# Attention in groups of two heads on the row halves of the tensor array, with the softmax denominators in spare columns of the value blocks

## The chip, the core and the metric

One core of one Trainium2 chip runs the kernel. Its engines are TensorE (PE: matmuls and transposes; PEld: loading of the stationary operand), VectorE (DVE), ScalarE (ACT), GpSimd (POOL) and SyncE (SP), which here only issues DMAs. The metric is the device time of one execution in microseconds; lower is better.

## What is computed

A decoder-like stack on x of shape 4 x 512 x 128: four layers, each a cross-attention to a context of 154 tokens and a feed-forward part, each with a residual and a LayerNorm ahead. The first three attentions have 16 heads of size 8; they are what the change touches.

```python
# layer 0 (layers 1 and 2: no memory keys; RMS-normed q and k, or rotary q and k)
K = concat([ctx @ Wk.T + bk, sqrt(8) * m_k])       # 154 context keys + 64 memory keys
V = concat([ctx @ Wv.T + bv, sqrt(64) * m_v])      # the value bias only on context keys
energy = einsum('bhqd,bhkd->bhqk', Qh, Kh) / sqrt(8)
energy[..., :154] = where(mask == 0, -1e20, energy[..., :154])
x = x + einsum('bhqk,bhkd->bhqd', softmax(energy), Vh) @ Wo.T + bo
```

Since the weights of a softmax add up to one, a constant vector added to all values comes out of the attention unchanged.

## The kernel before

The work is a list of 32 items in order, `ITEMS`: for each of 8 parts (A, F0, A, F1, A, F2, A3, F3) four items, one for each batch element b. A is an attention of 16 heads (layers 0, 1, 2), A3 the last attention, F0 to F3 the feed-forward parts. Every engine runs the same list in order. An item is cut into slots. `plan(i)` puts pieces for later items into the slots of item i: LayerNorm and projections of item i + 2 (`ln`, `norm`, `xt`, `q`, `kproj`), the transposed queries and keys, maxima and values of item i + 1 (`kt`, `kb`, `qxt`, `max`, `mt`, `v`), and the output projection of item i - 1 (`finish`). In a slot an engine first does the slot's own step, then the pieces in plan order. Nothing overtakes on an engine, and SP is one such queue as well: it processes `mt` (row copies), `w` (loads of feed-forward weights in chunks, at slots 4, 7, 10, ... of A items of layers 1 and 2) and `rows` in the same slot order.

An A item, before: heads are taken in 4 groups g of 4 heads. Keys lie in `KB` (97 rows: three parts of 8 for each of 4 heads, a bias row; 4 further rows for the negated maxima), queries in `QXT`, both float32r. The keys of a group are laid out as columns, head after head, cut into 7 chunks of 125 (layer 0) or 5 chunks of 124.
- `scores_for_max` (L725): 32 matmuls give scores with queries on partitions, 436 or 308 columns each, for two heads. DVE reduces each to negated maxima (`maxima`, L1100). Two PSUM banks, 2 and 3, take turns. `maxima_transposed` (L735), a copy by ACT (L1458) and four DMAs by SP (L492) bring the maxima into rows of `QXT`.
- `attention_step`: slot n computes scores of chunk n // 4 and group n % 4 with keys on partitions (L806, 512 columns) into bank n % 2; ACT exponentiates them into `P` (L1512). Four matmuls on column quarters of the array (a quad) multiply a chunk by the values into bank 6 (L817), four more by a 0/1 mask into bank 7 (L825), which gives the denominators on the same partitions as the values. There are N = 28 or 20 slots.
- `attention_end` (DVE): reciprocal of bank 7, 128 x 512 (L1219), times bank 6 (L1221). `attention_out`: output projection (L836) at slot 6 of a following A item or slot 2 of a feed-forward item, then the residual (L1228).
- `v_blocks` (L670, L673, L675): for each chunk the value projection of the context repeated four times (`ctx_rep`, loaded by a DMA for every item), a one-row matmul for the value bias, and in layer 0 the memory values.

Of the feed-forward parts, one step of F1 and F2 is two groups of three matmuls (L861 to L863) in a slot, followed by an activation on ACT and a product on DVE.

## Time and profile before

| | us |
|---|---|
| runs | 1133.59, 1137.58, 1139.87 |
| median | 1137.58 |
| profiled execution, its own time | 1143.49 |
| its span, first to last instruction | 1141.7 |
| PE busy | 1021.3 (89%) |
| DVE busy | 571.6 (50%) |
| ACT busy | 432.2 (38%) |
| POOL busy | 269.9 (24%) |

Busy time is a sum over the span; what bounds a stretch is read from that stretch. The mean granted TensorE clock was 0.918 of full speed. fp32 matmuls stand as two instructions in the trace, so a quad is eight rows.

### The profile page before, as it was taken

How to read it: one execution, taken by the hardware profiler on the slowest of the kernel's cores; microseconds unless marked ns; L12 is line 12 of the kernel's file. 1: busy time of each engine (PE TensorE's matmuls, PEld its weight loads, DVE VectorE, ACT ScalarE, POOL GpSimd, SP SyncE). 2: the span in 40 equal slices, each digit the busy share in tenths (PEclk: the TensorE clock that was granted, in tenths of full speed). 3: DMA queues.
4: the chain of work that ended last, by engine and by line, in shares of the span. 5: the costliest groups of instructions: out<-in, count | busy, mean ns of one | idle time of the engine just before them, and what ended most of it. 6: DMA issues, size and time to landing. Idle time of an engine off the chain costs nothing. (4 is left out here: it accounts for less than half of the span.)

```text
span 1141.7 us, 15533 instructions
## 1 busy us (share of the span) xinstructions
PE 1021.3 (89%) x5652; PEld 695.5 (61%) x5652; DVE 571.6 (50%) x1368; ACT 432.2 (38%) x777; POOL 269.9 (24%) x394
## 2 busy tenths in 40 slices
PE   2899999988789999989999989999989999999985
PEld 2644454336555544468887764544478888888774
DVE  3644645433345465454553445555464545444458
ACT  3164544343316445533242235553532323222240
POOL 8220112234415343310021013331210101000044
PEclk9889999787669899899999899889799999999997
DMA  5000000000010110000000011100000000000001
GB/s 137 3 1 13 1 13 2 12 1 16 1 68 1 32 31 2 30 20 1 1 1 1 1 40 43 44 25 15 26 6 1 1 1 1 1 1 1 1 1 38
DMA packets 27149, 18.11 MB, mean 16 GB/s; under 512 B 5793, under 2 KB 25345, under 8 KB 26946
## 3 DMA queue, kind: packets, MB, share of 16 engines
q1 hardware_dynamic: 27074, 17.12, 5.4%
q8 instruction: 46, 0.75, 0.3%
q14 instruction: 29, 0.24, 0.1%
HBM read 15.64 MB, written 1.05 MB: 15 GB/s over the span
## 5 line engine op out<-in xcount | busy, mean ns | idle before, releaser
L1100 DVE TENSOR_REDUCE mneg<-PS 128x2 f32<-128x308 f32 (+1 forms) x384 | 184.0, 517 | 167.7 <-PE PS L725 161.5
L1512 ACT ACTIVATE work<-PS 124x512 f32<-124x512 f32 (+1 forms) x272 | 160.1, 605 | 151.0 <-PE PS L806 150.3
L1246 DVE TENSOR_TENSOR work<-PS,work 128x512 f32<-128x512 f32 (+2 forms) x168 | 114.8, 685 | 175.4 <-PE PS L863 129.8
L1537 ACT ACTIVATE work<-PS 128x512 f32<-128x512 f32 (+2 forms) x168 | 99.9, 596 | 258.2 <-PE PS L863 245.9
L880 PEld LDWEIGHTS PS<-down_w,work 128*128 128x128 f32 (+2 forms) x1472 | 176.3, 195 | 6.3 <-DVE work L1246 1.3
L880 PE MATMUL PS<-down_w,work 128*128 128x128 f32 (+2 forms) x1472 | 176.2, 277 | 1.0 <-DVE work L1246 1.0
L861 PE MATMUL PS<-xh_sb,arena 128*128 128x512 f32 (+2 forms) x352 | 149.4, 424 | 10.4 <-DVE work L1246 9.6
L1607 POOL TENSOR_SCALAR rstd<-bn_mv 128x4 f32<-128x4 f32 x32 | 8.7, 271 | 585.3 <-DVE bn_mv L1024 585.1
L863 PE MATMUL PS<-xh_sb,arena 128*128 128x512 f32 (+2 forms) x352 | 142.5, 405 | 0.0
L862 PE MATMUL PS<-xl_sb,arena 128*128 128x512 f32 (+2 forms) x352 | 141.8, 403 | 0.0
L725 PE MATMUL PS<-kb_sb,qxt_sb 97*128 97x308 f32 x256 | 88.5, 393 | 19.8 <-DVE mneg L1100 15.6
L725 PEld LDWEIGHTS PS<-kb_sb,qxt_sb 97*128 97x128 f32 x256 | 46.8, 197 | 94.0 <-DVE mneg L1100 52.1
L861 PEld LDWEIGHTS PS<-xh_sb,arena 128*128 128x128 f32 (+2 forms) x352 | 66.1, 188 | 35.4 <-DVE work L1246 14.3
L817 PE MATMUL PS<-work,vb_sb 124*32 124x512 f32 (+1 forms) x544 | 80.3, 664 | 2.3 <-DVE work L1221 1.2
L806 PE MATMUL PS<-qxt_sb,kb_sb 101*124 101x512 f32 x160 | 74.9, 487 | 4.4 <-ACT work L1512 4.3
L863 PEld LDWEIGHTS PS<-xh_sb,arena 128*128 128x128 f32 (+2 forms) x352 | 66.1, 188 | 18.5
L825 PE MATMUL PS<-work,mv_sb 124*32 124x512 f32 (+1 forms) x544 | 76.4, 635 | 0.0
L862 PEld LDWEIGHTS PS<-xl_sb,arena 128*128 128x128 f32 (+2 forms) x352 | 66.3, 188 | 12.8
L1219 DVE RECIPROCAL work<-PS 128x512 f32<-128x512 f32 x12 | 40.3, 3357 | 43.4 <-PE PS L825 43.4
L1277 DVE SCALAR_TENSOR_TENSOR x_res<-PS,gates_sb,x_res 128x128 f32<-128x128 f32 x192 | 53.5, 339 | 5.9 <-PE PS L880 5.9
L1458 ACT ACTIVATE mt_sb<-PS 12x512 fp32r<-12x512 f32 (+1 forms) x24 | 14.1, 586 | 111.9 <-PE PS L735 111.8
L725 PE MATMUL PS<-arena,qxt_sb 97*128 97x436 f32 x128 | 48.9, 434 | 6.7 <-DVE mneg L1100 5.9
(168 smaller groups left out, 1301.6 us busy)
## 6 DMA issues: line engine op xcount, KB each, us to landing
ctx_rep<-in_ctxT SPq DMA_DIRECT2D x12, 308.0 KB, 3.3
stage<-in_w SPq DMA_DIRECT2D x8, 256.0 KB, 4.1
stage<-in_wg SPq DMA_DIRECT2D x8, 176.0 KB, 2.3
stage<-in_wu SPq DMA_DIRECT2D x8, 176.0 KB, 2.4
x_res<-in_x SPq DMA_DIRECT2D x4, 256.0 KB, 3.9
down_w<-in_w SPq DMA_DIRECT2D x1, 1024.0 KB
down_w<-in_wd SPq DMA_DIRECT2D x8, 128.0 KB
out<-x_res SPq DMA_DIRECT2D x4, 256.0 KB, 2.3
```

Of the source, the lines that this page charges most:

```text
L725: pe.matmul(PS[:, bank, 0:w], QXT[0:KX_ROWS, a % 2, g, t * 128:(t + 1) * 128], KB(layer)[0:KX_ROWS, a % 2, g, f * w:(f + 1) * w], start=Tr ...
L806: pe.matmul(PS[0:rows, n % 2, :], KB(layer)[0:K_ALL, a % 2, g, c * rows:(c + 1) * rows], QXT[0:K_ALL, a % 2, g, :], start=True, stop=True) ...
L817: pe.matmul(PS[32 * g:32 * g + 32, 6, :], VB[0:rows, a % 2, c, g * 32:(g + 1) * 32], P[0:rows, (4 * c + g) % P_RING, :], start=(c == 0), s ...
L825: pe.matmul(PS[32 * g:32 * g + 32, 7, :], mask[0:rows, c, :], P[0:rows, (4 * c + g) % P_RING, :], start=(c == 0), stop=(c == chunks - 1)). ...
L861: pe.matmul(o, w[0], xH[:, i % 2, :], start=True, stop=False)
L862: pe.matmul(o, w[0], xL[:, i % 2, :], start=False, stop=False)
L863: pe.matmul(o, w[1], xH[:, i % 2, :], start=False, stop=True).then_inc(*sig["up"].mark((i, kt, m)))
L880: mm = pe.matmul(PS[:, bank, t * 128:(t + 1) * 128], HH[0:rows, bank - 6, j, t * 128:(t + 1) * 128], rhs, start=(j == 0), stop=(j == len(t ...
L1100: dve.tensor_reduce(mneg[:, a % 2, t, h0:h0 + 2], PS[:, mx_bank(i_main, m), 0:2 * (KT0 if layer == 0 else KC)].rearrange("p (h n) -> p h n ...
L1246: dve.tensor_tensor(HH[0:rows, e % 2, j, :], PS[0:rows, 2 * (n % 2) + 1, :], SS[0:rows, n % 2, :], ALU.mult).then_inc(*sig["h"].mark((i, n)))
L1512: act.activation(P[0:rows, n % P_RING, :], PS[0:rows, n % 2, :], ACT.Exp, scale=SCALE).then_inc(*sig["p"].mark((i, n)))
L1537: act.activation(SS[0:rows, n % 2, :], PS[0:rows, bank, :], ACT.Silu).then_inc(*sig["act"].mark((i, n)))
```

## The change

Heads are taken in 8 half groups of 2 heads. Half group f of group g uses the rows 64 f to 64 f + 50 of the array (49 of them for the maxima), so that two matmuls, one on each row half, form a pair; each writes a PSUM bank of its own.

- An A item has N = 32 slots (layer 0: 4 chunks of 2 x 55 keys) or 24 (3 chunks of 2 x 52). At even slots stands a pair of scores (L851) into banks 0 and 1, and one exponential of 110 or 104 x 1024 from both (L1560). The next pair waits for it.
- Maxima: 16 pairs (L769) into banks 2 and 3 (4 and 5 in feed-forward items), one reduction of 880 or 624 values to 4 (L1148), and the next pair waits for it.
- Values: a half group has 32 columns in `VB`, 16 values, 2 columns of the mask (the denominators) and 14 zeros. One quad (L866) at every fourth slot, alternately into bank 6 and 7; no separate denominator matmuls.
- At slot N + 3 ACT evacuates both banks into `RAW` (128 x 1024, L1568). SP then issues 8 DMAs that bring the 16 denominator rows to `DEN` (128 x 64), 8 that bring the value rows to `VP`, and, after DVE's reciprocal of `DEN` (L1269), 8 that spread the reciprocals to `RB` (128 x 512). DVE multiplies `VP` by `RB` (L1275), and the output projection (L876) reads `VP`.
- In a following A item the reciprocal and its 8 DMAs stand at slot 2 (`recip`), the product at 6 (`normal`), the output projection at 8 (`finish`); in F0 at 0, 1, 2; in F1 and F2 at 1, 3, 4.
- The value bias is multiplied by the output weights once a layer (`value_bias`) and added to the output bias; the memory values have it subtracted. `ctx_rep` and its DMAs go; the context is loaded once with every column twice (`ctxR`, 128 x 1760 for 128 x 616).

```diff
-N_MAX = 2 * G * T
-P_RING = 8
-R0, C0 = 125, 7
-R1, C1 = 124, 5
...
+N_MAX = G * T
+P_RING = 4
+R0, C0 = 55, 4
+R1, C1 = 52, 3
...
         if is_attn(i - 1):
-            put(6, "finish", i - 1)
+            put(2, "recip", i - 1)
+            put(6, "normal", i - 1)
+            put(8, "finish", i - 1)
...
-            return (0, 1, 2, 3, 6, 7)[m % 6]
-        return (2 if ITEMS[i_main][0] == "A" else 4) + m % 2
+            return (0, 2, 6)[m % 3]
+        return 2 if ITEMS[i_main][0] == "A" else 4
...
+        def denominators_out(sp, i):
+            sp.wait_ge(*sig["raw"].at(i))
...
+            for j in range(2 * G):
+                bank, row = j // 4, 32 * (j % 4)
+                sp.dma_start(DEN[16 * j:16 * j + 16, :],
+                             RAW[row + 16:row + 18, bank, :].rearrange("p (s n) -> p s n", s=8)).then_inc(*sig["den_in"].more(i))
...
+            for j in range(2 * G):
+                bank, row = j // 4, 32 * (j % 4)
+                sp.dma_start(VP[16 * j:16 * j + 16, :], RAW[row:row + 16, bank, :]).then_inc(*sig["v_in"].more(i))
+        def reciprocals_out(sp, i):
+            sp.wait_ge(*sig["rden"].at(i))
...
+            for d in range(HD):
+                sp.dma_start(RB[d:128:HD, :].rearrange("p (s n) -> p s n", s=8), DEN[:, :]).then_inc(*sig["rden_in"].more(i))
...
+                    for f in range(2):
+                        if f in taken:
+                            pe.wait_ge(*taken[f])
+                        taken[f] = sig["p"].at((i, m))
+                    for f in range(2):
+                        mm = pe.matmul(PS[0:HB * rows, f, :], chunk_columns(layer, a % 2, g, f, c),
+                                       QXT[HALF * f:HALF * f + K_ALL, a % 2, g, :], start=True, stop=True)
...
-        def attention_end(i):
...
-            dve.reciprocal(ON, PS[:, 7, :]).then_inc(*sig["rden"].mark(i))
-            dve.tensor_tensor(ON, PS[:, 6, :], ON, ALU.mult).then_inc(*sig["on"].mark(i))
+        def reciprocals(i):
+            dve.wait_ge(*sig["den_in"].at(i))
+            dve.reciprocal(DEN[:, :], DEN[:, :]).then_inc(*sig["rden"].mark(i))
+        def normalise(i):
+            dve.wait_ge(*sig["v_in"].at(i))
+            dve.wait_ge(*sig["rden_in"].at(i))
+            dve.tensor_tensor(VP[:, :], VP[:, :], RB[:, :], ALU.mult).then_inc(*sig["on"].mark(i))
```

SP's queue, from the row copies for the third item of layer 1 (`qxt_sb<-mt_sb`) to its weight chunks (`stage<-in_w_1`). Before:

```order
L492 DMA qxt_sb<-mt_sb 4x512 x4
L485 DMA ctx_rep<-in_ctxT 128x4x154
L507 DMA stage<-in_w_1 128x512 x2
L492 DMA qxt_sb<-mt_sb 4x512 x4
L485 DMA ctx_rep<-in_ctxT 128x4x154
L507 DMA stage<-in_w_1 128x512 x2
```

Of the change:

```order
L503 DMA qxt_sb<-mt_sb 2x512 x8
L512 DMA den_sb<-raw_sb 16x1x64 x8
L518 DMA v_packed<-raw_sb 16x512 x8
L526 DMA rden_rows<-den_sb 16x8x64 x8
L541 DMA stage<-in_w_1 128x512 x2
L503 DMA qxt_sb<-mt_sb 2x512 x8
```

The weight chunks of an item stood behind its predecessor's row copies and one load; now 24 DMAs stand between.

PE, at the head of the second item of layer 1, up to behind the output projection of the item before it. Before:

```order
L650 MATMUL PS<-ident_sb,kx_sb 97x77 x8
L806 MATMUL PS<-qxt_sb,kb_sb 124x512 x2
L709 MATMUL PS<-ident_sb,qx_sb 97x128 x4
...
L806 MATMUL PS<-qxt_sb,kb_sb 124x512
L817 MATMUL PS<-work,vb_sb 32x512 x4
L725 MATMUL PS<-kb_sb,qxt_sb 128x308 x2
L806 MATMUL PS<-qxt_sb,kb_sb 124x512
L725 MATMUL PS<-kb_sb,qxt_sb 128x308 x2
L836 MATMUL PS<-w_attn,work 128x128 x4
L806 MATMUL PS<-qxt_sb,kb_sb 124x512
```

Of the change:

```order
L685 MATMUL PS<-ident_sb,kx_sb 115x78 x8
L851 MATMUL PS<-qxt_sb,kb_sb 104x512 x2
L749 MATMUL PS<-ident_sb,qx_sb 115x128 x4
...
L866 MATMUL PS<-work,vb_sb 32x512 x4
L769 MATMUL PS<-kb_sb,qxt_sb 128x312 x2
L851 MATMUL PS<-qxt_sb,kb_sb 104x512 x2
L769 MATMUL PS<-kb_sb,qxt_sb 128x312 x4
L851 MATMUL PS<-qxt_sb,kb_sb 104x512 x2
L769 MATMUL PS<-kb_sb,qxt_sb 128x312 x2
L876 MATMUL PS<-w_attn,v_packed 128x128 x4
L866 MATMUL PS<-work,vb_sb 32x512 x4
```

The output projection stands behind five pairs of scores (0 to 4) and four pairs of maxima, where it stood behind seven single scores and four maxima; seven pairs of scores follow it in the item.

DVE, in the same place, from the value mask to the residual. Before:

```order
L1052 TENSOR_TENSOR vb_sb<-PS,mv_sb 124x128
L1219 RECIPROCAL work<-PS 128x512
L1221 TENSOR_TENSOR work<-PS,work 128x512
L1022 BN_STATS bn_st<-x_res 128x6
L1024 BN_AGGR bn_mv<-bn_st 128x2
```

Of the change:

```order
L1269 RECIPROCAL den_sb<-den_sb 128x64
L1061 BN_STATS bn_st<-x_res 128x6
L1063 BN_AGGR bn_mv<-bn_st 128x2
L1148 TENSOR_REDUCE mneg<-PS 128x4 x2
L1275 TENSOR_TENSOR v_packed<-v_packed,rden_rows 128x512
L1148 TENSOR_REDUCE mneg<-PS 128x4 x2
L1282 TENSOR_TENSOR x_res<-PS,x_res 128x512
```

Reciprocal and product stood together ahead of the next item; now two maxima stand between them and two behind them, in the middle of the item.

## Rows read from the trace of the kernel before

**Rows 1.** The page: the span, and part 1, busy us, share and instructions.

```profile
span 1141.7 us, 15533 instructions
...
PE 1021.3 (89%) x5652; PEld 695.5 (61%) x5652; DVE 571.6 (50%) x1368; ACT 432.2 (38%) x777; POOL 269.9 (24%) x394
```

**Rows 2.** Windows, an attention item each: length; busy PE, PEld, DVE, ACT, POOL; PEclk, DMA.

```profile
58.70:108.30 49.60, 46.75 (x269) 25.10 (x270) 21.68 (x38) 23.58 (x44) 7.38 (x9) 0.95 0.03 8
108.30:157.40 49.10, 45.48 (x270) 23.34 (x269) 26.91 (x48) 23.59 (x43) 7.39 (x9) 1.00 0.03 8
157.40:208.00 50.60, 46.67 (x250) 22.14 (x248) 26.26 (x50) 22.18 (x41) 12.53 (x24) 0.93 0.03 8
208.00:240.70 32.70, 29.49 (x143) 9.79 (x142) 11.71 (x19) 17.52 (x33) 12.64 (x24) 0.84 0.01 2
...
342.20:384.00 41.80, 39.34 (x209) 21.64 (x209) 20.89 (x50) 20.23 (x37) 19.09 (x38) 0.87 0.07 21
384.00:424.50 40.50, 37.85 (x209) 20.18 (x209) 23.25 (x55) 20.14 (x38) 19.07 (x38) 0.91 0.02 5
424.50:462.10 37.60, 33.75 (x189) 16.29 (x187) 20.82 (x47) 18.61 (x35) 9.52 (x13) 1.00 0.07 22
462.10:484.60 22.50, 20.39 (x107) 8.71 (x106) 11.25 (x25) 13.69 (x28) 9.67 (x13) 0.85 0.12 38
...
679.40:722.00 42.60, 39.63 (x196) 20.08 (x197) 19.47 (x41) 20.58 (x40) 14.85 (x18) 0.84 0.24 69
722.00:762.00 40.00, 37.80 (x209) 20.14 (x209) 23.17 (x51) 20.84 (x40) 15.74 (x19) 0.91 0.07 18
762.00:802.80 40.80, 37.25 (x185) 17.06 (x183) 20.63 (x46) 18.59 (x35) 7.10 (x8) 0.89 0.11 33
802.80:824.90 22.10, 21.52 (x103) 9.09 (x102) 10.84 (x24) 13.60 (x29) 7.80 (x9) 0.74 0.07 17
```

**Rows 3.** Groups by line and shape: busy us, mean ns, idle before.

```profile
L1100 DVE TENSOR_REDUCE mneg<-PS 128x2 f32<-128x308 f32 x256 | 111.5, 473 | 114.8 <-PE PS L725 109.5
L1100 DVE TENSOR_REDUCE mneg<-PS 128x2 f32<-128x436 f32 x128 | 72.5, 605 | 52.9 <-PE PS L725 52.0
L817 PE MATMUL PS<-work,vb_sb 124*32 124x512 f32 x320 | 48.7, 683 | 1.2 <-DVE work L1221 0.6 <-ACT work L1512 0.5
L673 PE MATMUL PS<-b_v,ind_sb 1*124 1x128 f32 x80 | 22.9, 372 | 0.0
```

**Rows 4.** Timeline: start, duration us, engine, line; end of layer 0, then 418.74.

```profile
236.79 0.73 PE L806 MATMUL PS<-qxt_sb,arena 101*125 101x512 f32 x2
237.32 1.08 ACT L1512 ACTIVATE work<-PS 125x512 f32<-125x512 f32 x2 [0.57 <-PE PS L806]
...
237.45 1.07 PE L817 MATMUL PS<-work,vb_sb 125*32 125x512 f32 x8
...
238.44 0.73 PE L806 MATMUL PS<-qxt_sb,arena 101*125 101x512 f32 x2
...
418.74 1.93 PE L817 MATMUL PS<-work,vb_sb 124*32 124x512 f32 x8
```

**Rows 5.** SP's issues: one tile's (ns, min/median/max), then the timeline, and who waits.

```profile
L492 SPq DMA_DIRECT2D qxt_sb<-mt_sb x48: 584/585/700, 53.8 to 799.7; - x48
...
255.15 0.58 SPq L515 DMA_DIRECT2D qb_sb<-xn_sb  x1
255.78 0.58 SPq L516 DMA_DIRECT2D qb_sb<-xn_sb  x1
...
257.46 1.03 POOL L1713 TENSOR_TENSOR stage<-qb_sb,eye_sb 4x512 f32<-4x512 f32 x1 [3.55 <-DMA qb_sb<-xn_sb]
```

**Rows 6.** The page, part 6: weight chunks, KB and us from issue to landing.

```profile
stage<-in_wg SPq DMA_DIRECT2D x8, 176.0 KB, 2.3
```

**Rows 7.** Timeline: around the end of layer 1's last attention item.

```profile
484.60 1.06 PE L817 MATMUL PS<-work,vb_sb 124*32 124x512 f32 x8 [0.54 <-ACT work L1512]
...
492.96 1.06 PE L836 MATMUL PS<-w_attn,work 128*128 128x128 f32 x8
```

More of the change, by code:

```diff
@@ L99, in weight_chunks, with last_pair, last_quad, last_attention @@
     return [(m, e * F2, F2) for e in range(E2) for m in range(2)] + [(m, E2 * F2, FS) for m in range(2)]
+def last_pair(i):
+    return n_slots(i) // 2 - 1
+def last_quad(i):
+    return n_slots(i) // 4 - 1
+def last_attention(i):
+    return max(n for n in range(i) if ITEMS[n][0] == "A")
 def last_expert(kind):
@@ L139, in plan @@
                 put(0, "kt", a1)
-            for h in range(HL):
+            for h in range(HB):
                 put(h, "kb", a1, h)
@@ L180, in plan @@
             put(0, "kt", a1)
-            for h in range(HL):
+            for h in range(HB):
                 put(0, "kb", a1, h)
@@ L655, in v_blocks @@
[L655 removed]
+                taken[4] = taken[5] = sig["kb"].at((a, HB - 1))
+            def v_blocks(a):
                 layer, b = a // B, a % B
                 rows, chunks = chunk_shape(layer)
[L659 to L673 removed]
+                if a == 0:
+                    pe.wait_ge(*sig["mem_ready"].at(0))
+                    pe.wait_ge(*sig["const_in"].at(0))
+                pe.wait_ge(*taken[4])
+                for c in range(chunks):
+                    o = PS[0:HB * rows, 4, c * D:(c + 1) * D]
+                    cols = slice(c * HB * rows, (c + 1) * HB * rows)
+                    mem = layer == 0 and (c + 1) * rows > KP
+                    mm = pe.matmul(o, ctxR[:, b, cols], WA[:, layer % 2, 2, :], start=True, stop=not mem)
@@ L809, in attention_step @@
                 if n % 4 == 1 and n >= 5:
[L810 to L811 removed]
+                    u = (n - 5) // 4
+                    c, bank = u // 2, 6 + u % 2
+                    pe.wait_ge(*sig["p"].at((i, 2 * u + 1)))
                     if c == 0:
[L813 to L818 removed]
@@ L819, in attention_step @@
-                if n % 4 == 3 and n >= 7:
-                    c = (n - 7) // 4
-                    mask = MV0 if layer == 0 else MV1
-                    if c == 0 and 7 in taken:
-                        pe.wait_ge(*taken[7])
-                    for g in range(G):
-                        pe.matmul(PS[32 * g:32 * g + 32, 7, :], mask[0:rows, c, :], P[0:rows, (4 * c + g) % P_RING, :],
-                                  start=(c == 0), stop=(c == chunks - 1)).then_inc(*sig["dn"].mark((i, 4 * c + g)))
-                    if c == chunks - 1:
-                        taken[6] = taken[7] = sig["on"].at(i)
+                        if u == 0:
+                            pe.wait_ge(*sig["vb"].at(a))
@@ new lines, in attention_step @@
+                        if bank in taken:
+                            pe.wait_ge(*taken[bank])
+                        taken[bank] = sig["raw"].at(i)
+                    for r in range(4):
+                        j = 4 * (u % 2) + r
+                        mm = pe.matmul(PS[32 * r:32 * r + 32, bank, :], VB[0:HB * rows, a % 2, c, j, :], P[0:HB * rows, j // 2, j % 2, :],
+                                       start=(c == 0), stop=(c == chunks - 1))
+                    mm.then_inc(*sig["pv"].mark((i, u)))
@@ L1566, in _ @@
             q_split(0)
-            for h in range(HL):
+            for h in range(HB):
                 kb_out(0, h)
```

478 lines of the change are left out of this document (235 added, 243 removed).

## The prediction

> **What bounds the kernel now.** I read the page's busy times first, then the windows cut at the first exponential of each attention item, then the groups by shape, then two short pieces of the timeline. TensorE is busy for 1021.3 of 1141.7 us [rows 1]; no other engine passes 50%. The twelve attention items take 470 us of the span [rows 2]: 49 to 51 us each in layer 0, 38 to 43 us in layers 1 and 2, and the last item of each layer, which carries no maxima for a following attention, 32.7, 22.5 and 22.1 us up to its last exponential. Inside them TensorE is busy over 90% of the time while DVE and ACT stand at about half: there TensorE's instruction stream is the bound, and DVE and ACT have room. SP issues four small DMAs for an item and is idle otherwise. The last item of a layer is different: [rows 4] shows two scores at 236.79, their exponentials from 237.32 for 1.08 us, and the next two scores at 238.44. That is a loop of 1.65 us through ACT, not TensorE's own work.
>
> **What the change takes off TensorE.** (a) Denominator products (L825) go, and the value products become quads of 4 matmuls over 110 or 104 keys: layer 0 has 8 quads where 7 + 7 stood, layers 1 and 2 have 6 where 5 + 5 stood. A quad takes 1.0 us ([rows 4], 1.07 with its tail; the 40 value quads of layers 1 and 2 in [rows 3] are 48.7 us of busy time, 1.2 each, slow ones among them). That is 6 us less for an item of layer 0 and 4 us for the others, 56 us in all. (b) Value projection: the bias rows (L673, two instructions of 0.29 us each in [rows 3]) go, and there are 4 or 3 blocks instead of 7 or 5: some 5 and 3 us an item, 44 us. (c) 32 maxima matmuls become 16 pairs on row halves, 28 or 20 score matmuls become 16 or 12 pairs. Whether halves run side by side no row shows: a pair costs between one matmul and two. I take one and a bit (0.3 to 0.4 us), since the groups of four on column quarters, the nearest case in the trace, do overlap [rows 4]. So about 100 us of TensorE work leave the attention items without doubt. If nothing replaced it, this would be the gain.
>
> **Loop lengths that take its place.** Every pair now fills both banks it has, so nothing is double-buffered. Scores to exponentials: 0.53 + up to 1.08 (1024 columns in one instruction; it may save 0.1) + 0.04 = 1.55 to 1.65 us a pair [rows 4]: 16 x 1.6 = 25.6 us in layer 0, 12 x 1.6 = 19.2 us in the others, against 14 x 1.65 and 10 x 1.65 before. Maxima: one reduction over 880 or 624 values. From 0.473 us for 308 and 0.605 us for 436 [rows 3] each value adds 1.03 ns, giving 1.06 and 0.80 us; with about 0.5 us from matmul to reduction (as scores to exponentials) and 0.04 back the loop is 1.6 and 1.35 us, and 16 of them are 26 and 22 us. ACT also has 2 key copies and 4 query copies at an item's head, so the first maxima come some 7.5 us in, and after the last one stand the value blocks, a quad and two groups of transposes, 3.5 to 4.5 us. Undisturbed, an item with maxima is then 7.5 + 15 x 1.35 + about 1.5 (projections queued between the maxima) + 3.5 = 33 us in layers 1 and 2, and 7.5 + 15 x 1.6 + 2 + 4.5 = 38 us in layer 0. Only the first item of each layer is undisturbed: 49.6 to 38, 41.8 and 42.6 to 33: **-30 us**.
>
> **What the change adds to the path.** The denominators no longer leave PSUM through one DVE reciprocal but through SP: 8 DMAs for denominators, 8 for the values, 8 for the reciprocals, all queued on SP in this order (the first order piece of the section on the change). An SBUF-to-SBUF issue holds SP for 0.584 to 0.585 us and the next starts 0.63 us after it [rows 5]; the last of a set has landed 1.7 us after its issue begins (255.78 to 257.46). Counted from the end of the evacuation, T: denominators issued by T+5.0, landed T+6.2, reciprocal done T+6.6; values issued until T+10.1, and only then SP reaches the reciprocals, whose last issue begins at T+14.5 and lands at T+16.2; the product (0.69, as L1221 before) is done at T+17. The next item's first score stands about 1.1 us before T, since the evacuation (up to 1.08 us) waits behind a 4-row copy on ACT. TensorE wants this product at slot 8, ahead of pair 5, which it reaches about 10 us into the item. **It waits there until about 18 us.** Queued behind it are all later scores, maxima and quads; ACT and DVE then wait for those. DVE meets the same chain earlier: its reciprocal stands at slot 2, its product at slot 6 behind two maxima, so nothing of DVE's can help. In layers 1 and 2 SP's weight loads for slots 4 and 7 (second order piece) now stand behind the reciprocals: issued at T+15.1, landed about 2.3 later [rows 6], copied by ACT by 19 us into the item. Exponential 3 and those behind it wait for that, so pair 4 starts at 20 us.
>
> **The sum, item by item.**
> - Layer 0, second and third: slot 8 at 18.1, one product of 0.8, 13 maxima x 1.6, queued work of 2.3, tail 4.5: 46.5 each against 49.1 and 50.6: **-7**.
> - Layers 1 and 2, second and third: 20 + 13 x 1.35 + 3 + 3.5 = 44 each against 40.5, 37.6, 40.0 and 40.8: **+17**.
> - Last items: layer 0 18.1 + 0.8 + 1 + 11 x 1.6 = 37.5 against 32.7; the others 20 + 0.5 + 8 x 1.6 = 33 against 22.5 and 22.1 (first score to last exponential): **+5 and +21**.
> - The FFN items that follow them: their copy of this wait stands at slot 2 (F0) or 4 (F1, F2). Before, the output projection came 6 to 8 us after the last exponential (492.96 against 484.60 [rows 7]); now T is 2.2 us after it and the wait ends at 19. F0 +13; in F1 and F2 two more steps of FFN matmuls, 3 us, run ahead of it: +8.5 each: **+30**.
> - F0 and F1 items that prepare an attention: half the maxima matmuls and fewer value blocks, but single-buffered: -6. Prologue: 17 us of reductions for 19.4, shorter value projection, larger context load ahead of the weights: -3 (between -6 and +3). **-9**.
>
> Sum: -30 - 7 + 17 + 26 + 30 - 9 = +27 us against the profiled execution's 1141.7 (1143.5 with what lies around it), 1169 for the same span. The median of the runs shown is 1137.6, 5.9 below that execution, so I forecast **1165 us**. The value bias moved into the output bias costs one matmul and one small addition a layer, at an item's start: nothing.
>
> **One rule weighed.** [rows 5] shows each issue at 0.58 us, one after the other, for four rows of 0.5 to 2 KB: eight of them cost 5 us before the last has begun. The Trainium skill, "DMA: Bandwidth & Descriptors", section "Issuing engines are not separate DMA queues", says that the sequencer time to initiate a DMA "is usually small relative to the DMA itself". By that rule the three sets would cost little more than three landings, about 6 us, which is rival 1. The trace speaks against it.
>
> **Rivals.** (1) **The chain is hidden.** Were issues cheap, the product would be ready 6 us after T, before slot 8: no item would be held, all would run at 38 and 33 us, the last ones at 26.5 and 20: -30 - 24 - 27 - 11 + 3 - 9 = -98, about 1040 us. It decides at the issue time: twelve chains share the +27, so a chain 2.3 us shorter (0.53 us an issue for 0.63) is break-even. Against it stand 48 issues between 584 and 700 ns [rows 5]. (2) **TensorE's queue is quicker than I reckon**, each loop 0.2 us shorter because exponential and reduction of double width save more of their fixed part: about 150 loops, -30 us, 1135 us. Nothing in the trace has these widths. (3) **Issues of many short rows cost more**: the reciprocal DMAs move 128 pieces of 256 bytes; 0.25 us more on 16 of the 24 is 4 us on twelve chains, +48, 1213 us. (4) **Row halves do not overlap, or the clock is low after each 8 us pause**: a quad took 1.93 us at 418.74 [rows 4] where it takes 1.07 at the full clock; +0.15 us on each loop, or 2 to 3 us after each of twelve pauses, is about +30, 1195 us.
>
> **How the numbers follow.** Forecast 0.52 (1140 to 1190 by the bounds above), rival 1 0.10, rival 2 and the lower edge of the forecast 0.18, rival 3 0.10, rival 4 0.10. The range 1115 to 1210 leaves out rival 1 and the upper part of rival 3. Within 0.5%, about what a measurement here can tell from no change, is 1132 to 1143: 0.13. Faster: rival 1 and half of rival 2, 0.22. Slower: 0.65.
>
> **What would show it.** Right: SP busy with 24 issues of 0.63 us after each attention item; TensorE idle 6 to 8 us before the output projection in 9 attention items and 3 FFN items, released by DVE's product, which was released by a DMA; first items of layers at 38 and 33 us; the granted clock at 1.2 GHz for a while behind each pause. Wrong: issues of 0.3 us or less, an output projection that waits for nothing, or score pairs that follow each other in under 1.4 us.

## The result and the profile after the change

The changed kernel takes 1274.3 us (median of 4 runs, 1269.8 to 1281.2) against 1137.2 us (median of 4 runs) on the same chip: a ratio of 1.121, 95% interval 1.115 to 1.127. The forecast was 1165 us, up to 1210. The sign was right, and the loss (137 us) is five times the 28 us that were forecast. Some runs of any of these kernels fall into a slower state with a lower granted clock; comparisons are between the others, of which e9_split has only one.

From the page of the changed kernel (span 1279.4 us): each engine's busy time, the granted clock in 40 slices (tenths of full speed), and the chain that ended last.

```profile
PE 988.2 (77%) x5034; PEld 651.6 (51%) x5034; DVE 518.2 (41%) x1167; ACT 439.6 (34%) x649; POOL 263.0 (21%) x375
PEclk9566666657855665568999995665558999999997
PE 60%; SPq 15%; DVE 11%; ACT 5%; issue 5%; DMA 3%; POOL 1%; DVEq 0%; ACTq 0%; POOLq 0%
```

Two things stand out. SP's queue is 15% of the chain (the page of the kernel before follows its own chain back over 1 or 2% of the span only, so there is no share to set beside it). And the granted clock, 7 to 9 tenths in all but two slices before, is 5 to 7 tenths wherever attention items run. TensorE's busy time fell by only 33 us (1021.3 to 988.2), though by the forecast's count about 100 us of work were taken from it: what is left takes longer.

The windows of the changed kernel, cut as in [rows 2], columns as there. Four of layer 0, the stretch of FFN0, four of layer 1, the stretch of FFN1, and from the last item of layer 2 to the end.

```profile
53.60:105.80 52.20, 44.48 (x199) 20.86 (x200) 20.04 (x26) 24.07 (x31) 5.61 (x7) 0.62 0.00 1
105.80:164.70 58.90, 43.83 (x199) 19.87 (x198) 22.13 (x30) 23.92 (x32) 7.38 (x9) 0.62 0.05 11
164.70:222.70 58.00, 39.92 (x176) 17.09 (x174) 23.13 (x32) 22.04 (x28) 12.53 (x24) 0.62 0.05 11
222.70:266.50 43.80, 28.77 (x106) 9.05 (x106) 8.88 (x21) 18.08 (x21) 12.59 (x23) 0.59 0.06 14
266.50:384.10 117.60, 71.56 (x315) 50.25 (x315) 37.30 (x80) 27.67 (x45) 36.06 (x53) 0.69 0.04 9
384.10:429.40 45.30, 39.63 (x167) 19.82 (x168) 18.24 (x34) 21.17 (x29) 18.99 (x38) 0.55 0.10 36
429.40:483.30 53.90, 35.35 (x167) 17.22 (x167) 19.73 (x37) 20.67 (x29) 19.14 (x38) 0.65 0.08 21
483.30:536.00 52.70, 37.64 (x146) 16.48 (x146) 17.18 (x29) 19.36 (x26) 9.55 (x13) 0.52 0.08 21
536.00:574.10 38.10, 19.65 (x86) 8.18 (x86) 7.16 (x19) 14.44 (x19) 9.17 (x12) 0.61 0.11 29
574.10:768.20 194.10, 174.45 (x1058) 147.10 (x1058) 93.38 (x235) 62.00 (x99) 22.04 (x23) 0.97 0.02 6
...
916.70:956.80 40.10, 22.12 (x82) 8.16 (x82) 8.03 (x18) 15.08 (x21) 7.81 (x9) 0.50 0.13 33
956.80:1279.40 322.60, 294.77 (x1764) 248.47 (x1764) 163.75 (x466) 96.20 (x175) 39.11 (x44) 0.96 0.02 6
```

Every attention item is longer than before, the undisturbed first ones too (52.2 against 49.6, 45.3 against 41.8), at a clock of 0.50 to 0.65 where [rows 2] has 0.74 to 1.00. A granted clock of 0.50 is the lower of TensorE's two levels, 1.2 GHz, all the time, and 1.00 the higher, 2.4 GHz. The FFN1 stretch and the last one run close to the higher one (0.97 and 0.96), and FFN0 has 0.69; the same stretches of the kernel before have 0.96, 0.97 and 0.72.

The chain of DMAs is where the forecast put it. The second item of layer 1 starts at 429.4; its timeline, some rows left out (start, duration, engine and line, in brackets the idle time before and who ended it):

```profile
429.84 5.31 SPq L512 DMA_DIRECT2D den_sb<-raw_sb  x8
...
435.20 5.00 SPq L518 DMA_DIRECT2D v_packed<-raw_sb  x8
...
436.30 0.55 DVE L1269 RECIPROCAL den_sb<-den_sb 128x64 f32<-128x64 f32 x1 [9.28 <-DMA den_sb<-raw_sb]
...
440.30 5.09 SPq L526 DMA_DIRECT2D rden_rows<-den_sb  x8
445.43 1.06 SPq L541 DMA_DIRECT2D stage<-in_w  x2
446.77 0.69 DVE L1275 TENSOR_TENSOR v_packed<-v_packed,rden_rows 128x512 f32<-128x512 f32 x1 [7.44 <-DMA rden_rows<-den_sb]
...
448.49 0.63 ACT L1513 ACTIVATE arena<-stage 128x512 fp32r<-128x512 f32 x1 [12.92 <-DMA stage<-in_w]
...
450.18 0.75 PE L851 MATMUL PS<-qxt_sb,kb_sb 51*104 51x512 f32 x2 [8.12 <-ACT work L1560]
```

The 24 issues fill SP from 429.84 to 445.39, the product is done at 447.46, 17.6 us after they began; the weight load, queued behind them, lets ACT go on at 448.49, and TensorE has waited 8.1 us for the exponential behind that copy.

What the forecast did not have is in the loops. From the first item of layer 1, where no chain disturbs (rows in between left out):

```profile
393.03 0.63 PE L769 MATMUL PS<-kb_sb,qxt_sb 49*128 49x312 f32 x2
...
404.70 0.41 PE L769 MATMUL PS<-kb_sb,qxt_sb 49*128 49x312 f32 x2
...
406.10 0.41 PE L769 MATMUL PS<-kb_sb,qxt_sb 49*128 49x312 f32 x2 [0.75 <-DVE mneg L1148]
406.44 1.06 PE L866 MATMUL PS<-work,vb_sb 104*32 104x512 f32 x8
...
409.60 0.63 PE L769 MATMUL PS<-kb_sb,qxt_sb 49*128 49x312 f32 x2 [0.68 <-DVE mneg L1148]
...
411.22 0.63 PE L769 MATMUL PS<-kb_sb,qxt_sb 49*128 49x312 f32 x2 [0.34 <-DVE mneg L1148]
...
411.78 1.93 PE L866 MATMUL PS<-work,vb_sb 104*32 104x512 f32 x8
411.89 0.81 DVE L1148 TENSOR_REDUCE mneg<-PS 128x4 f32<-128x624 f32 x1 [0.81 <-PE PS L769]
...
413.65 0.63 PE L769 MATMUL PS<-kb_sb,qxt_sb 49*128 49x312 f32 x2
...
422.95 0.63 PE L769 MATMUL PS<-kb_sb,qxt_sb 49*128 49x312 f32 x2 [1.00 <-DVE mneg L1148]
```

The reduction takes 0.81 us, as reckoned (0.80). The two row halves run side by side: two matmuls in 0.41 us, no longer than the one of before. But from 407 us on a pair takes 0.63 us and a quad 1.93 instead of 1.06. The loop of 1.40 us (404.70 to 406.10; 1.35 was reckoned) becomes 1.62 (409.60 to 411.22), and 2.43 us (411.22 to 413.65) where a quad stands in it: at 1.06 us the quad lies beside DVE's work (after the one at 406.44 the next pair still waits 0.36 us for DVE), at 1.93 it sticks out by 0.8. The first and the last row are the first and the sixteenth pair of maxima of the item: 15 loops in 29.9 us.

### The profile page after: what moved, and what is told of

It reads as the page before. It is cut to its first block, busy times and chain, and to the rows that moved or that the text cites. A ratio compares the mean times of both kernels' runs of the same rounds, so it can differ in the third digit from the quotient of the medians.

```text
span 1279.4 us, 14562 instructions
## 1 busy us (share of the span) xinstructions
PE 988.2 (77%) x5034; PEld 651.6 (51%) x5034; DVE 518.2 (41%) x1167; ACT 439.6 (34%) x649; POOL 263.0 (21%) x375
## 4 chain that ended last, share of the span: by engine, by line
PE 60%; SPq 15%; DVE 11%; ACT 5%; issue 5%; DMA 3%; POOL 1%; DVEq 0%; ACTq 0%; POOLq 0%
PE PS L920 13%; PE PS L866 9%; DVE mneg L1148 6%; PE PS L901 6%; PE PS L769 6%; PE PS L903 6%; PE PS L902 6%; SPq L512 5%; SPq L518 5%; SPq L526 4%; PE PS L851 4%; ACT work L1560 2%; PE PS L876 2%; PE PS L779 1%; PE PS L702 1%
## 5 line engine op out<-in xcount | busy, mean ns | idle before, releaser
L1148 DVE TENSOR_REDUCE mneg<-PS 128x4 f32<-128x624 f32 (+1 forms) x192 | 170.6, 894 | 205.4 <-PE PS L769 205.2
L1560 ACT ACTIVATE work<-PS 104x1024 f32<-104x1024 f32 (+1 forms) x160 | 163.5, 1022 | 185.7 <-PE PS L851 184.0
L866 PE MATMUL PS<-work,vb_sb 104*32 104x512 f32 (+1 forms) x640 | 140.5, 967 | 3.4 <-ACT work L1560 3.4
L851 PE MATMUL PS<-qxt_sb,kb_sb 51*104 51x512 f32 x192 | 62.8, 642 | 74.0 <-ACT work L1560 72.4
L769 PE MATMUL PS<-kb_sb,qxt_sb 49*128 49x312 f32 x256 | 69.1, 527 | 60.1 <-DVE mneg L1148 54.5
L769 PEld LDWEIGHTS PS<-kb_sb,qxt_sb 49*128 49x128 f32 x256 | 36.0, 259 | 127.8 <-DVE mneg L1148 94.9
L851 PEld LDWEIGHTS PS<-qxt_sb,kb_sb 51*104 51x104 f32 x192 | 23.7, 230 | 105.5 <-ACT work L1560 91.3
L876 PE MATMUL PS<-w_attn,v_packed 128*128 128x128 f32 x96 | 24.8, 440 | 45.1 <-DVE v_packed L1275 30.9
L769 PE MATMUL PS<-arena,qxt_sb 49*128 49x440 f32 x128 | 38.3, 600 | 25.0 <-DVE mneg L1148 25.0
```

The lines of the kernel that those rows point to most:

```text
L769: mm = pe.matmul(PS[:, bank + f, 0:w], QXT[half, a % 2, g, t * 128:(t + 1) * 128], KB(layer)[half, a % 2, g, 0:w], start=True, stop=True)
L851: mm = pe.matmul(PS[0:HB * rows, f, :], chunk_columns(layer, a % 2, g, f, c), QXT[HALF * f:HALF * f + K_ALL, a % 2, g, :], start=True, sto ...
L866: mm = pe.matmul(PS[32 * r:32 * r + 32, bank, :], VB[0:HB * rows, a % 2, c, j, :], P[0:HB * rows, j // 2, j % 2, :], start=(c == 0), stop= ...
L1148: dve.tensor_reduce(mneg[:, a % 2, t, g * HL:(g + 1) * HL].rearrange("p (f h) -> p f h", f=2), PS[:, bank:bank + 2, 0:HB * head_width(laye ...
L1560: act.activation(P[0:rows, m % P_RING, :, :], PS[0:rows, 0:2, :], ACT.Exp, scale=SCALE).then_inc(*sig["p"].mark((i, m)))
```

## The experiments

Eleven kernels, each beside runs of the kernel before on its own chip. "Ratio" is against those.

**1. The chain moved later (e1_late).** The changed kernel with other slot numbers for the chain, and for the weight loads that queue behind it on SP:

```diff
-            put(2, "recip", i - 1)
-            put(6, "normal", i - 1)
-            put(8, "finish", i - 1)
+            put(10, "recip", i - 1)
+            put(16, "normal", i - 1)
+            put(18, "finish", i - 1)
...
-                put(4 + 3 * (c - b * n_w // B), "w", layer, c)
+                put(9 + 3 * (c - b * n_w // B), "w", layer, c)
...
-            put(0 if short else 1, "recip", i - 1)
-            put(1 if short else 3, "normal", i - 1)
-            put(2 if short else 4, "finish", i - 1)
+            put(0 if short else 2, "recip", i - 1)
+            put(4 if short else 8, "normal", i - 1)
+            put(5 if short else 10, "finish", i - 1)
```

> The changed kernel with its chain of DMAs moved later, nothing left out: in an attention item the reciprocal stands at slot 10, the product at 16 and the output projection at 18 (2, 6 and 8 before), the weight loads of layers 1 and 2 begin at slot 9 instead of 4; in the FFN entries product and projection stand at slots 4 and 5 (F0), 8 and 10 (F1, F2). Theory A (the chain of 24 SP issues holds TensorE, as forecast): the held items shrink to the length of the first item of their layer: layer 0 58.9 and 58.0 to 52, layer 1 54.0 and 52.7 to 45, layer 2 53.4 and 50.8 to 44, last items 43.8, 38.1, 40.1 to 37, 31, 31, FFN entries 5 us each: 85 us less, about 1190 us; still 50 us over the kernel before, since the undisturbed items are 3 us too long even then. Theory B (the loops and a TensorE clock at its lower level set the length, the chain mostly lies beside them): held work comes back elsewhere, not more than 30 us less, 1245 us. If the clock follows TensorE's share of busy time, taking the pauses away raises the granted clock above 0.6 in these items and the gain passes 100 us.

Measured: 1189.2 us (1181.8 to 1190.8), ratio 1.045 (1.036 to 1.053), 85 us less than the changed kernel. Windows of this kernel: first item of layer 0, first and second of layer 1, last of layer 1, the FFN1 stretch.

```profile
53.90:103.30 49.40, 41.70 (x199) 19.99 (x200) 20.40 (x28) 24.06 (x31) 7.16 (x10) 0.66 0.00 1
...
354.50:399.70 45.20, 39.52 (x167) 19.73 (x168) 18.62 (x36) 21.22 (x29) 20.63 (x41) 0.55 0.10 36
399.70:443.90 44.20, 32.14 (x167) 16.05 (x168) 19.86 (x37) 20.73 (x30) 18.17 (x38) 0.73 0.11 26
...
489.20:519.80 30.60, 22.44 (x86) 8.74 (x86) 5.02 (x17) 14.59 (x19) 7.33 (x10) 0.55 0.14 36
519.80:701.30 181.50, 170.94 (x1058) 144.80 (x1058) 93.64 (x235) 61.80 (x99) 22.13 (x23) 1.00 0.02 6
```

The second item of layer 1 falls from 53.9 to 44.2, about the length of the undisturbed first; the last from 38.1 to 30.6; FFN1 from 194.1 to 181.5. Theory A holds: the chain costs the change at least 85 us. At least, because it has not left the path everywhere. In this same second item TensorE still waits 4.8 us (up to 427.67) for an exponential that stands behind a weight chunk queued on SP behind the reciprocals, in FFN0 5.7 us (up to 265.47) for the product, and the second item of layer 2 takes 52.7 us, hardly less than in the changed kernel (53.4), where 44 had been expected. The run also says that the chain is not all: 1189 is some 50 us above the kernel before (by the ratio; the runs that it is compared with have a median of 1140.4), and the first item of layer 1 did not change (45.3 and 45.2).

**2. The values' copies on the POOL queue (e5_vpool).** The eight issues of a set go to another queue, the chain stays at its slots:

```diff
-                    sp.dma_start(VP[16 * j:16 * j + 16, :], RAW[row:row + 16, bank, :]).then_inc(*sig["v_in"].more(i))
+                    pool.dma_start(VP[16 * j:16 * j + 16, :], RAW[row:row + 16, bank, :]).then_inc(*sig["v_in"].more(i))
```

> The changed kernel, nothing left out, with the chain at its slots but the eight copies of the values issued from the POOL queue instead of SP's. Theory A (the 24 issues one after the other on SP set when the product is ready): SP reaches the reciprocals 5 us earlier, product at about T+12 instead of T+17, the weight loads 5 us earlier: 5 us less on nine held attention items and three FFN entries, 60 us less than the changed kernel's 1274 (or 45 where a part of it is taken up by other waits): 1215 to 1230 us. Theory B (the landings set it, not the issues, or POOL issues slower than SP): within 15 us of the changed kernel. If an issue on POOL costs 1.1 us instead of 0.63, the eight take 9 us and still end before T+12: nothing is lost unless POOL's own work is late.

Measured: 1234.9 us (1228.9 to 1236.7), ratio 1.085 (1.078 to 1.092): 39 us less. The timeline of its second item of layer 0:

```profile
99.52 4.13 POOL L1764 DMA_DIRECT2D v_packed<-raw_sb  x8 [5.29 <-ACT raw_sb L1563]
99.56 5.29 SPq L512 DMA_DIRECT2D den_sb<-raw_sb  x8
...
106.59 5.46 SPq L521 DMA_DIRECT2D rden_rows<-den_sb  x8
...
113.42 0.69 DVE L1270 TENSOR_TENSOR v_packed<-v_packed,rden_rows 128x512 f32<-128x512 f32 x1 [2.88 <-DMA rden_rows<-den_sb]
```

The reciprocals' issues begin 7.0 us after the first issue, and the product ends at 14.6 us. The same item of the changed kernel has 11.1 and 18.2 us. In the second item of layer 1 the product ends at 14.6 us again, 17.6 in the changed kernel. 3.0 to 3.6 us less on twelve chains is 36 to 43 us, about what was measured. I had reckoned 5: SP is free after 5.3 us, but then waits for DVE's reciprocal, which the longer queue had hidden. So the issues, one after the other, are the greater part of the price of this chain: 15.5 of the 17.6 us in the changed kernel.

**3. One part of the change alone (e4_bias).** The kernel before, with the value bias joined to the output bias and nothing else:

```diff
-                    pe.matmul(o, CR[:, a % 2, cols], WA[:, layer % 2, 2, :], start=True, stop=False)
-                    ind = IND0[:, cols] if layer == 0 else IND0[:, 0:rows]
-                    mm = pe.matmul(o, ind, BVr[:, layer, :], start=False, stop=not mem)
+                    mm = pe.matmul(o, CR[:, a % 2, cols], WA[:, layer % 2, 2, :], start=True, stop=not mem)
...
+                pe.matmul(PS[:, 5, 0:D], BVc[:, layer:layer + 1].to_broadcast([128, 128]), WA[:, layer % 2, 3, :],
+                          start=True, stop=True).then_inc(*sig["bv_psum"].mark(layer))
```

> The kernel before with one part of the change alone: the value bias goes into the output bias (one matmul and one addition a layer), the 136 one-row matmuls of the value projection are gone. They were 0.29 us apart on TensorE, which bounds the items that hold them. If that time counts fully: 136 x 0.29 = 39 us less, 1098 us. If part of it lies beside other waits (the value projection of the last FFN0 and FFN1 items, whose TensorE waits elsewhere), and the clock falls a little where TensorE has less to do: 20 us less, 1117 us. A rival (the item's length is set by DVE and ACT as well, and the gap is filled by waits for maxima and exponentials): within 5 us of the kernel before.

Measured: 1089.9 us (1085.3 to 1090.5), ratio 0.959 (0.950 to 0.967). Its first two items of layer 0 and the first of layer 1:

```profile
57.90:103.30 45.40, 42.67 (x255) 22.62 (x256) 21.71 (x37) 23.59 (x44) 7.38 (x9) 0.95 0.03 7
103.30:148.20 44.90, 41.27 (x255) 20.80 (x254) 26.97 (x48) 23.62 (x44) 7.39 (x9) 1.00 0.03 9
...
319.70:356.30 36.60, 34.45 (x199) 19.20 (x200) 20.35 (x52) 20.20 (x37) 19.11 (x38) 0.92 0.13 46
```

These three items are 4.2, 4.2 and 5.2 us shorter than in [rows 2]. By the ratio the kernel takes 47 us less. What went are 68 one-row matmuls, 136 instructions in the trace (the text of the expectation counts the instructions as matmuls), so 0.35 us an instruction. Their own rows account for less: 22.9 us for 80 of them ([rows 3], 0.29 each, what I had reckoned with) and 14.0 for the other 56, 37 us together. The other 10 us are not separated; the granted clock of the three items went from 0.95, 1.00 and 0.87 to 0.95, 1.00 and 0.92, and that of the whole kernel rose from 0.92 to 0.94. This part of the change gains 4% and is the fastest kernel of the study.

**4. The clock raised by matmuls with zeros (e2_late_fill, e3_fill, e8_late_fill1).** Behind each pair of maxima matmuls, three (in e8_late_fill1 one) of this:

```diff
+                    for _ in range(3):
+                        pe.matmul(PS[:, 6 if m < 4 else 7, 0:128], zero[:, :], ident[:, :], start=False, stop=False)
```

> As e1_late, and behind each pair of maxima matmuls of an attention item three matmuls of 128 columns that multiply by a tile of zeros and add into the bank of the values (nothing in the result changes): 0.64 us more of TensorE work each at the full clock, in the time in which DVE reduces. Theory A (TensorE fell to the lower clock because it had become idle between its matmuls): the granted clock in the attention items goes from 0.6 to over 0.85, a quad from 1.93 to 1.06 us; 8 or 6 quads an item give 5 to 7 us, transposes and projections 2 us, the maxima loops 1 to 2 us: 9 us on each of nine items and 4 on the last ones, about 90 us less than e1_late, 1100 us. Theory B (single banks set the length whatever the clock): the clock may rise, but the time stays within 15 us of e1_late. Theory C (the clock doesn't answer to such matmuls): 144 x 1.28 us at the lower clock, partly beside DVE: 50 us more than e1_late.

> The changed kernel with its chain where it was and the same zero matmuls behind each maxima pair. Theory A (clock from idleness): the pauses of 8 us in front of the output projection remain, so the clock rises only in parts of an item; 40 to 60 us less than the changed kernel's 1274, some 1220 us. Theory B (single banks): 1260 to 1290 us. Theory C: over 1300 us.

> As e2_late_fill with one zero matmul of 128 columns behind each pair of maxima matmuls in place of three. In e2_late_fill the granted clock rose from 0.55 or 0.65 to 0.9 and the first item of layer 1 fell from 45.2 to 39.7 us, but TensorE was busy for 98% of it: the zero matmuls themselves had become its bound. If one is enough to keep the clock up: 0.6 us less on each of 144 pairs, 1150 us. If one is too little: the clock stays near 0.6 and the time at e1_late's 1189. In between 1170.

Measured: 1190.4, 1267.7 and 1199.4 us; ratios 1.047 (1.039 to 1.056), 1.114 (1.105 to 1.123) and 1.054 (1.046 to 1.062). None can be told from the same kernel without zeros (1189.2 for e2_late_fill and e8_late_fill1, 1274.3 for e3_fill): the intervals overlap each time, though e8_late_fill1 stands 10 us above. Windows of e2_late_fill, first item of layer 0 and of layer 1:

```profile
53.60:103.60 50.00, 49.36 (x294) 30.80 (x295) 20.49 (x28) 24.04 (x30) 6.01 (x9) 0.84 0.01 2
...
350.90:390.60 39.70, 39.04 (x264) 26.70 (x265) 18.44 (x36) 20.72 (x28) 19.39 (x40) 0.93 0.11 42
```

The clock does answer, 0.66 to 0.84 and 0.55 to 0.93, and the item of layer 1 gains 5.5 us. But TensorE is now busy for 98% of it: the zeros have filled it up themselves. By its time the experiment stays inconclusive; it only says that the clock can be moved.

**The clock's price without any edit.** The first item of layer 0 runs the same instructions in the changed kernel, in e1_late and in e5_vpool, at three clocks: 52.2 us at 0.62, 49.4 at 0.66, and in e5_vpool

```profile
53.60:99.10 45.50, 37.37 (x198) 19.13 (x199) 20.03 (x26) 23.71 (x30) 5.68 (x7) 0.76 0.01 1
```

DVE's and ACT's busy times are the same in all three (20.0 to 20.4, 23.7 to 24.1); TensorE's are 44.5, 41.7 and 37.4. So 6.7 us of this item are the clock's alone. A fixed part and a part that goes with one over the clock, from the two ends: 6.7 / (1/0.62 - 1/0.76) = 22.6, and 45.5 - 22.6/0.76 = 15.8; the middle one would be 50.0 (measured 49.4). At the full clock this estimate gives 38.4 us, and the forecast had 38. It reaches beyond what was measured: no run has this item above 0.76, and a part that waits for DVE or ACT would not shrink further.

**5. Single banks in the kernel before (e6_single).** Nothing of the change; only its way of using PSUM:

```diff
-            return (2 if ITEMS[i_main][0] == "A" else 4) + m % 2
+            return 2 if ITEMS[i_main][0] == "A" else 4
...
-                    pe.matmul(PS[0:rows, n % 2, :], KB(layer)[0:K_ALL, a % 2, g, c * rows:(c + 1) * rows],
+                    pe.matmul(PS[0:rows, 0, :], KB(layer)[0:K_ALL, a % 2, g, c * rows:(c + 1) * rows],
```

> The kernel before, nothing left out and nothing of the change in it, except that scores always use bank 0 (0 and 1 in turn before) and the maxima matmuls bank 2 or 4 (2 and 3, or 4 and 5, in turn before). Theory D (one set of banks in place of two is what makes the changed kernel's undisturbed items too long, and the clock follows from the waits): a maxima loop becomes 0.41 + 0.25 + 0.40 + 0.04 = 1.1 us, 32 of them 35 us instead of the 24 they take now in layers 1 and 2, 1.2 us and 38 instead of 31 in layer 0: 9 us on nine items; the last items, 1.15 us a score instead of 0.83: 22 us in all; the FFN items that prepare an attention 5 us each; about 110 us, 1250 us, with a granted clock in the attention items near 0.6 instead of 0.9, which adds to it. Rival (TensorE always finds other work in its stream, so that one bank suffices): under 40 us more and a clock that stays over 0.8.

Measured: 1501.3 us (1494.9 to 1510.7), ratio 1.319 (1.308 to 1.329): 362 us more, three times what waits had been reckoned to give. First item of layer 0 and of layer 1:

```profile
60.40:146.90 86.50, 76.61 (x268) 35.36 (x268) 23.99 (x39) 24.27 (x44) 7.36 (x9) 0.60 0.02 5
...
490.80:565.20 74.40, 63.42 (x209) 29.73 (x207) 22.57 (x51) 20.55 (x37) 18.68 (x38) 0.55 0.04 12
```

The clock falls from 0.95 to 0.60 and from 0.87 to 0.55, and TensorE's busy time grows from 46.8 to 76.6 us with no work added. Of the 36.9 us that the item of layer 0 grew by, 29.9 are such longer busy time and 7.0 idle time; TensorE's waits for the maxima's bank went from 1.6 to 9.4 us.

**6. The same with zeros between (e12_single_fill).** e4_bias, single banks, one matmul by zeros behind each maxima matmul.

> The kernel e4_bias (before, value bias joined to the output bias) with single banks for scores and maxima as in e6_single, and one matmul of 128 columns by zeros behind each maxima matmul of an attention item; nothing left out. e6_single took 362 us more than the kernel before, three times what waits alone were reckoned to give, at a granted clock of 0.55 to 0.74 in its attention items. Without the zero matmuls this kernel would be 1501 - 48 = about 1450 us. Theory E (most of those 362 us are the clock): clock at 0.9, items back near 55 us in layer 0 and 45 in layers 1 and 2, 1250 us. Rival (most are waits for the bank): the clock may rise, and the time stays within 50 us of 1450.

Measured: 1315.4 us (1308.4 to 1326.4), ratio 1.149 (1.137 to 1.160), against about 1450 without the zeros. That 1450 is an estimate (1501 - 48): no kernel with single banks and the joined bias ran without them. It may be some 20 us too high, since the one-row instructions cost more at the low clock (14 of them 5.5 us in e6_single's first item, 3.4 before). The same two items:

```profile
57.60:122.60 65.00, 58.34 (x318) 34.09 (x318) 23.19 (x40) 24.35 (x45) 7.38 (x9) 0.87 0.02 5
...
411.00:467.80 56.80, 48.58 (x262) 28.84 (x262) 21.92 (x53) 20.44 (x37) 18.72 (x38) 0.87 0.08 29
```

Against that estimate added work made the kernel 115 to 135 us faster, and the first items are 65.0 and 56.8 us for e6_single's 86.5 and 74.4. At least that part of the loss of e6_single is the clock; the 1250 us of theory E were not reached, and what stands in between was not separated (the waits for a bank and the zeros themselves remain). So in the kernel before, single banks bring waits, the lower clock comes with them, and it costs more than the waits. That the changed kernel's low clock starts the same way is not shown by this.

**7. The pairs undone (e9_split, e10_late_split, e11_late_split_fill).** In the changed kernel and in e1_late each row half gets its own wait, its own bank and its own exponential or reduction, so that one bank is filled while the other is read:

```diff
-                    mm.then_inc(*sig["st"].mark((i, m)))
+                    if f in taken:
+                        pe.wait_ge(*taken[f])
+                    taken[f] = sig["p"].at((i, n))
+                    pe.matmul(PS[0:HB * rows, f, :], chunk_columns(layer, a % 2, g, f, c),
+                              QXT[HALF * f:HALF * f + K_ALL, a % 2, g, :], start=True, stop=True).then_inc(*sig["st"].mark((i, n)))
```

> The changed kernel, chain at its slots, nothing left out, with the pairing undone and the rest kept: the two row halves of a score step and of a maxima step are issued one by one, each into its own bank with its own exponential (512 columns) or reduction (312 or 440 values), so that one bank is filled while the other is read. Theory D (a pair that fills both banks is what makes TensorE wait, and the lower clock follows): the undisturbed items shrink to what TensorE's stream needs at the full clock, 35 us in layers 1 and 2 and 43 in layer 0 (before: 41.8 and 49.6 with two to six more quads and the bias rows); the held ones keep the chain, 18 to 20 us into the item, and gain 6 us each behind it: 75 us less, about 1200 us, granted clock 0.75 in the items. Theory B (the small matmuls of the row halves lower the clock or cost as much as whole ones): within 20 us of 1274.

> e1_late (chain of DMAs moved later) and e9_split in one, nothing left out. If the chain (85 us, measured) and the shared banks are the two causes and nothing else is wrong with the change, this kernel must come out below the kernel before: items of 43 us in layer 0 and 35 in layers 1 and 2 against 49.8 and 40.5: 9 x 6 = 55 us less, last items 4 us longer each (32 or 24 exponentials for 28 or 20), FFN entries and prologue as before: about 1095 us, near e4_bias (1090), granted clock in the items 0.9. If a third cause is there (strided reductions, narrower blocks, POOL or ACT), it stays at 1140 or above.

> As e10_late_split (chain later, pairs undone), and two matmuls of 128 columns by zeros behind each maxima step of an attention item; nothing left out. In e10_late_split TensorE was busy for 95% of the items of layer 0 and still had a granted clock of 0.55 to 0.62 there: so idleness is not what lowers the clock in it. Theory E (the row halves, narrow as they are, keep the clock at its lower level even back to back, and the level is what costs the time): with the zero matmuls on the whole array the clock comes back to 0.9, each pass of 0.63 us becomes 0.4 and each quad 1.06: items of 44 us in layer 0 and 36 in layers 1 and 2 although 16 x 0.6 us of zero matmuls are added, 1130 us in all, 95 less than e10_late_split. Rival (TensorE's stream itself is too long): the clock rises and the added matmuls eat it up: 1200 to 1230 us. Theory C (the clock does not answer): 1260 us or more.

Measured: e9_split 1288.9 us (one run), e10_late_split 1227.7 (1224.0 to 1231.2; ratio 1.075, 1.064 to 1.085), e11_late_split_fill 1277.8 (1266.7 to 1281.2; ratio 1.116, 1.107 to 1.125). None goes the way theory D wanted: e9_split's one run is 15 us above the changed kernel, e10_late_split 38 above e1_late, and e11_late_split_fill 50 more again with the zeros. Theory D as I had put it falls. The first two items of layer 0 in e10_late_split:

```profile
54.90:108.80 53.90, 51.03 (x200) 24.00 (x201) 21.41 (x44) 25.91 (x47) 6.47 (x9) 0.62 0.00 1
108.80:165.90 57.10, 53.59 (x198) 23.80 (x197) 23.08 (x46) 25.16 (x47) 8.12 (x11) 0.55 0.05 11
```

and TensorE's groups in the first one, of e10_late_split (scores, maxima) and then of the changed kernel:

```profile
L847 PE MATMUL PS<-qxt_sb,arena 51*110 51x512 f32 x33 | 15.9, 601 | 0.3 <-ACT work L1558 0.3
L768 PE MATMUL PS<-arena,qxt_sb 49*128 49x440 f32 x32 | 15.1, 595 | 2.6 <-DVE mneg L1145 2.5
```

```profile
L851 PE MATMUL PS<-qxt_sb,arena 51*110 51x512 f32 x32 | 9.7, 596 | 1.3 <-ACT work L1560 1.3
L769 PE MATMUL PS<-arena,qxt_sb 49*128 49x440 f32 x32 | 9.6, 588 | 6.5 <-DVE mneg L1148 6.5
```

Two halves that start together cost one; apart they cost 0.6 us each at this clock (0.62), and 11.7 us more in this item. The waits did go (6.5 to 2.6 us), and TensorE is busy for 94 and 95% of these items, yet its clock stays at 0.62 and 0.55, where the kernel before, as busy (46.75 of 49.60 and 45.48 of 49.10 us), had 0.95 and 1.00. e11_late_split_fill shows both within one kernel, the first item of layer 0 and the third of layer 2:

```profile
55.30:109.20 53.90, 53.84 (x264) 30.57 (x264) 21.45 (x44) 26.09 (x46) 6.31 (x9) 0.78 0.01 1
...
855.40:916.00 60.60, 59.26 (x206) 32.22 (x206) 17.72 (x44) 20.80 (x37) 5.51 (x7) 0.50 0.09 22
```

100% and 98% busy, at 0.78 and 0.50. So TensorE's idle time alone does not explain a low clock in kernels built on row halves, and what does is left open. A high busy share is no sign of a dense stream either: the low clock itself stretches it (the same instructions were busy for 37.4 us at 0.76 and 44.5 at 0.62).

## Why the forecast was wrong

Point by point, by its own steps.

- **The chain: right.** 24 issues of 0.63 us, product done 17.6 us after they began (T+17), exponential 3 at 19.6 us and pair 4 at 20.8 us into the second item of layer 1 (20), output projection held to 21.7 (18 to 20). Rival 1 falls: e5_vpool takes out a third of the issues from SP and gains 39 us, e1_late moves them mostly off the path and gains 85. Between forecast and rival 1 lay 125 us (+27 and -98); the runs show that the chain costs at least 85. The FFN entries were forecast at +30; e1_late takes 7.8, 12.6 and 9.2 us off the three stretches, 29.6. The Trainium skill, "DMA: Bandwidth & Descriptors", section "Issuing engines are not separate DMA queues", calls the sequencer's time to initiate a DMA usually small relative to the DMA itself. Here one issue takes 0.63 us, a third of the 1.9 to 2.0 us from issue to landing, and 24 in a row 15.5 us; the measurement decides.
- **TensorE's work taken off: right, and understated for the bias.** The one-row matmuls alone gave 47 us (e4_bias; 37 by their own rows); the forecast had 44 us for the whole value projection.
- **Row halves: the first half of rival 4 falls.** A pair takes 0.41 us at the full clock, as one whole matmul did. The Trainium skill, "TensorEngine Tiling (Array Packing)", section "Theoretical Speedup", gives up to 2x for a small dimension of at most 64; the trace agrees, as long as both halves start together (apart, in e10_late_split, they gain nothing).
- **Loop lengths: the step that failed.** They were added up from durations at the full clock, with the quads between them taken at nothing, to 38 us (layer 0) and 33 us (layers 1 and 2) for an undisturbed item. Measured: 52.2, 45.3 and 44.3 for the three first items, 38 us too much together. The six held items with maxima came out 59 us over the forecast (58.9, 58.0, 53.9, 52.7, 53.4 and 50.8 for 46.5 and 44) and the three last ones 18 us (43.8, 38.1 and 40.1 for 37.5 and 33). Prologue and FFN stretches were 5 us better than forecast. That is 115 - 5 = 110 us, and the span is 1279.4 for a forecast 1168.7.
- **What stood in its place.** In layer 0 the clock is 6.7 us of the 14.2 by measurement and nearly the whole by estimate: the same instructions give 52.2, 49.4 and 45.5 us at 0.62, 0.66 and 0.76, which leads to 38.4 at the full clock. In layers 1 and 2 it is at least 5.5 of 12.3 us (e2_late_fill, zeros counted against it). Where those 12.3 us lie, the rows of the first item of layer 1 show: its first maxima stand 8.9 us in (7.5 reckoned), the sixteenth 29.9 us later (21.8, 15 loops of 1.35 and 1.5 for projections), and the item ends 6.5 us after that (3.5). Two thirds are in the loops. The lower clock acts twice: a loop grows by its longer matmul (1.62 for 1.40 us), and a quad of 1.93 us no longer fits beside DVE's 0.81.
- **Rival 4 named the mechanism and put 30 us on it.** It let the clock be low behind each pause of 8 us. It is low from the first item of a layer on, where there is no such pause: the longest wait of TensorE in the first item of layer 1 is 1.0 us, and its clock is 0.55. I had the granted clock of [rows 2] before me (0.84, 0.85 and 0.74 in the last items, bound by the loop through ACT, against up to 1.00 elsewhere), and did not ask what it would be when every item is turned into such a loop.
- **Why the gain of 100 us of TensorE's work did not come.** Taken alone, the bias gives 47 of them (e4_bias: 1090 us). The changed kernel stands 184 us above that: at least 85 are the chain; the other 99, from e4_bias to e1_late on one chip, are all the rest of the change together: pairs with single banks at the lower clock, and what e1_late still waits for the chain. No run parts them.
- **Left open.** Whether single banks start the fall of the clock in the changed kernel as they do in the kernel before (e6_single), or the row halves hold it down by themselves (e10_late_split). Undoing the pairs was meant to tell, and changed both.

## What to carry to other kernels

Where an engine has two clock levels, reckon a new loop at both before counting work taken off as a gain. Here the lower one was the nearer in nearly every item whose loops had come to run through another engine's wait, and also in items on row halves in which TensorE was busy for 94% and more. Count the instructions that issue a chain of small DMAs, at the issue time of the trace, before the landings; and put what waits for such a chain as late as its consumer allows, since a few slot numbers were worth 85 us here; look too at what queues behind the chain (here weight loads). Time the parts of a bundled change one by one: here the smallest was a gain of 4%, hidden under the others, which lost four times as much.
